# A Mamba-style scan block with attention and experts on one core: the exponent's "+ 1" on GpSimd, two matmul groups cut in thirds, two scan buffers exchanged and ten row loads issued earlier

## The reference

```python
x = x + L0(_gn(x), ...)            # group norm, then a 2-D selective scan
t = t + L1_attn(_ln_t(t), ...)     # linear attention (no softmax)
t = t + L1_ffn(_ln_t(t), ...)      # top-1 routing to 8 experts

# L0, B=4 images of 32x32 pixels, 384 channels, DI=192, N=16 states, K=4 directions
xz = x @ in_proj_w.T;  xh, z = split(xz)
xc = silu(depthwise_conv3x3(xh) + conv_b)
xs = stack(rows, columns, flipped rows, flipped columns)
dts, Bs, Cs = split(einsum(xs, x_proj_w))
dts = softplus(einsum(dts, dt_projs_w) + dt_projs_b)
h = h * exp(d_t * A) + (d_t * u_t) * B_t        # 1024 steps, for each of 16 states
y = sum_n h * C_t
...                                             # norm, gate by silu(z), out_proj
```

## Time and profile before

| what | value |
|---|---|
| median of 3 runs | 2448.16 us (2448.04 to 2449.8) |
| the profiled execution | 2452.28 us, its span 2450.4 us |
| busy: PE, DVE, ACT, POOL | 2047.7, 1642.5, 1139.7, 1283.9 us |
| mean granted clock of TensorE | 0.933 |
| first scan starts at | 306.38 us |

### The profile page before, as it was taken

One profiled execution on the slowest core, in us unless ns is written; L12 is line 12 of the kernel. 1 busy time (PEld: TensorE's weight loads), 2 busy tenths in 40 slices (PEclk: granted clock), 3 DMA queues, 4 the chain that ended last, 5 costly groups with the idle time before them and its releaser, 6 DMA issues.

```text
span 2450.4 us, 20397 instructions
## 1 busy us (share of the span) xinstructions
PE 2047.7 (84%) x5854; PEld 954.6 (39%) x5854; DVE 1642.5 (67%) x1531; ACT 1139.7 (47%) x1228; POOL 1283.9 (52%) x455
## 2 busy tenths in 40 slices
PE   7977478888888888888888888668999599999998
PEld 3432123333333333333333333225665255555554
DVE  5686899999999999999999999474455200000000
ACT  2675756666666666666666666121121111111111
POOL 0101089999999999999989999000133111111110
PEclk9987589999999999999999999788999799999999
DMA  5554533222432223322223220401122633322210
GB/s 202 183 191 126 201 99 81 60 60 60 104 89 60 60 60 102 90 61 60 60 77 94 68 69 17 194 26 39 52 78 99 246 115 116 113 107 101 99 61 6
DMA packets 78848, 231.96 MB, mean 95 GB/s; under 512 B 10783, under 2 KB 37009, under 8 KB 76880
## 3 DMA queue, kind: packets, MB, share of 16 engines
q1 hardware_dynamic: 72656, 214.39, 27.8%
q0 software_dynamic: 6144, 16.98, 1.9%
HBM read 169.24 MB, written 64.03 MB: 95 GB/s over the span
## 4 chain that ended last, share of the span: by engine, by line
PE 44%; DVE 31%; issue 15%; ACT 6%; DMA 1%; DVEq 1%; POOL 0%; SPq 0%; ACTq 0%; POOLq 0%
DVE arena L1469 16%; PE ps L1249 10%; PE ps L1261 10%; PE ps L1010 7%; DVE ps L1462 6%; ACT ps L725 3%; PE ps L999 3%; PE ps L1198 3%; PE ps L914 2%; DVE arena L1335 1%; PE ps L941 1%; PE ps L1149 1%; PE ps L1187 1%; PE ps L1127 1%; PE ps L1059 1%
## 5 line engine op out<-in xcount | busy, mean ns | idle before, releaser
L537 POOL TENSOR_TENSOR arena<-arena 128x2048 f32<-128x2048 f32 x192 | 869.1, 4527 | 85.7 <-DVE arena L1469 85.7
L1010 PE MATMUL ps<-arena 128*128 128x512 f32 x1536 | 763.7, 621 | 29.0 <-DVE arena L1439 25.6
L1469 DVE TENSOR_TENSOR_SCAN arena<-arena,ps 128x1024 f32<-128x1024 f32 x264 | 603.7, 2287 | 44.9 <-DVE ps L1462 23.3
L999 PE MATMUL ps<-arena 96*128 (+1 forms) x1296 | 358.9, 393 | 214.4 <-DVE arena L1469 193.1
L730 ACT ACTIVATE arena<-ps 128x1024 f32<-128x1024 f32 x384 | 391.3, 1019 | 307.8 <-PE ps L999 304.6
L1010 PEld LDWEIGHTS ps<-arena 128*128 128x128 f32 x1536 | 303.9, 199 | 297.3 <-issue 233.8
L520 POOL TENSOR_TENSOR arena<-arena 128x1024 f32<-128x1024 f32 x120 | 283.1, 2359 | 101.2 <-DMA arena<-b_rows 101.2
L999 PEld LDWEIGHTS ps<-arena 96*128 96x128 bf16 x1296 | 119.3, 100 | 545.4 <-DVE arena L1469 302.4
L1462 DVE TENSOR_TENSOR ps<-ps,arena 128x1024 f32<-128x1024 f32 x264 | 319.0, 1208 | 8.2 <-PE ps L999 5.2
L1761 DVE TENSOR_TENSOR arena<-ps,arena 128x384 f32<-128x384 f32 x32 | 17.9, 558 | 450.0 <-PE ps L1261 450.0
L725 ACT ACTIVATE arena<-arena 128x1024 f32<-128x1024 f32 x264 | 300.8, 1140 | 26.1 <-DVE arena L1469 22.4
(11 more groups left out here) (202 smaller groups left out, 1670.6 us busy)
## 6 DMA issues: line engine op xcount, KB each, us to landing
arena<-b_rows SPq DMA_DIRECT2D x240, 256.0 KB, 7.5
arena<-in_w SPq DMA_DIRECT2D x16, 2304.0 KB
delta<-arena SPq DMA_DIRECT2D x24, 512.0 KB, 2.9
delta_x<-arena SPq DMA_DIRECT2D x24, 512.0 KB, 3.7
arena<-delta SPq DMA_DIRECT2D x24, 512.0 KB, 3.6
arena<-delta_x SPq DMA_DIRECT2D x24, 512.0 KB, 4.6
arena<-in_xT SPq DMA_DIRECT2D x6, 1536.0 KB, 9.6
slot_in<-arena SPq DMA_DIRECT2D x8, 772.0 KB, 14.0
```

The costliest lines, as they stand in the source:

```text
L537: nc.gpsimd.tensor_tensor(hst[:, h:h + 2], hst[:, h:h + 2], c_sb[:, c:c + 2], ALU.mult).then_inc(p2_ok, 2)
L999: mm = pe.matmul(dst[:, h * 512:(h + 1) * 512], sel_lhs[0:BR, n], bc[0:BR, q % OJ // J, dr, m, h * 512:(h + 1) * 512], start=True, stop=True)
L1010: mm = pe.matmul(Y_PS[:, h * 512:(h + 1) * 512], ident, hst[:, u % HRING, h * 512:(h + 1) * 512], start=(u == 0), stop=(u == UN - 1))
L1469: nc.vector.tensor_tensor_scan(h, f, x, 0.0, ALU.mult, ALU.add).then_inc(sc_ok, 1)
```

## The change

1. `one_more` of every half moves to POOL, as a `tensor_scalar` from `u_mk` to `w_mk`. ACT loses twelve instructions and DVE twelve.
2. `in_proj` loops over the thirds outside and the halves inside, and with j = 0 waits for each third of the normalised image by itself. `x_proj(p, 0)` likewise waits for each of the three `conv_out` by itself.
3. ACT loads the table for sqrt ahead of its first wait for data.
4. `hst` and `c_sb` exchange places. DVE now waits for `bc_st` alone; ACT waits for `rows_st` before unit 0, and for the last delta stores (`dm_st`) before it copies C of unit 3.
5. SP issues the first five B rows, ten DMAs, after the stores of the last half but one of pair 1, ahead of the last half's two stores.

```diff
-        c_sb, hst = rs.take(RING, S), rs.take(HRING, S)
+        hst, c_sb = rs.take(HRING, S), rs.take(RING, S)
...
                     store_delta(p, i)
+                    if p == 1 and i == HALVES - 2:
+
+                        sp.wait_ge(z_st, 32 * NP)
+                        for u in POOL_UNITS[:XRING]:
+                            b_row(0, u)
...
-            sp.wait_ge(z_st, 32 * NP)
-            for k in range(2):
-                sp.wait_ge(bc_st[k], K * NP // 2 * PLACED)
-                sp.wait_ge(rows_st[k], K * NP // 2 * 16)
-            for i in range(MADE):
-                sp.wait_ge(dm_st[i], NP * HALVES // MADE * 32)
...
+            def one_more(p, i):
+                m = p * HALVES + i
+                pool.wait_ge(u_ok, m + 1)
+                if m >= 2:
+                    pool.wait_ge(pd_ok, m - 1)
+                nc.gpsimd.tensor_scalar(w_mk[p][:, m % 2], u_mk[:, m % MADE], 1.0, None, ALU.add).then_inc(w_ok, 1)
+
             for p in range(NP):
                 for j in range(J):
                     by_columns(p, j)
+                for s in range(HALVES):
+                    one_more(p, s)
...
+            nc.scalar.preload_act_table_set("sqrt_and_others")
             group_std(0)
...
-                        if s % 2 == 0:
-                            one_more(p, s)
...
+                    if first and u == 3:
+                        for i in range(MADE):
+                            act.wait_ge(dm_st[i], NP * HALVES // MADE * 32)
                     nc.scalar.activation(c_sb[:, u % RING], C_PS, ACT.Copy).then_inc(c_free, 1)
...
             act.wait_ge(z_st, 32 * NP)
-            act.wait_ge(pd_ok, NP * HALVES)
-            act.wait_ge(split_ok, 2 * K * NP)
+            for k in range(2):
+                act.wait_ge(rows_st[k], K * NP // 2 * 16)
...
-                if j == 0:
-                    pe.wait_ge(xn_ok, im + 1)
                 slot = slot_free("in", im, j)
-                for h in range(2):
-                    for t in range(CT):
+                for t in range(CT):
+                    if j == 0:
+                        pe.wait_ge(xn_ok, im * CT + (t + 1))
+                    for h in range(2):
...
-                for h in range(2):
-                    for j in range(J):
+                for j in range(J):
+                    if k == 0:
+                        pe.wait_ge(ev_free, p * FILLS + IN_P + (j + 1))
+                    for h in range(2):
...
-                if i % 2:
-                    dve.wait_ge(u_ok, m + 1)
-                    if m >= 2:
-                        dve.wait_ge(pd_ok, m - 1)
-                    chain.link(nc.vector.tensor_scalar(w, u, 1.0, None, ALU.add))
-                else:
-                    dve.wait_ge(w_ok, m // 2 + 1)
+                dve.wait_ge(w_ok, m + 1)
...
-            for i in range(MADE):
-                dve.wait_ge(dm_st[i], NP * HALVES // MADE * 32)
             for k in range(2):
                 dve.wait_ge(bc_st[k], K * NP // 2 * PLACED)
-                dve.wait_ge(rows_st[k], K * NP // 2 * 16)
```

More of the change, by code:

```diff
@@ L389, in load_delta, with b_row @@
                 sp.dma_start(dux[:, dr], du_dram[q * 2 + dr]).then_inc(du_ld[dr], 16)
+            def b_row(q, u):
+                dr, n = divmod(u, N)
+                x = q * len(POOL_UNITS) + pool_units(u)
+                if x >= XRING:
+                    old_q, old = divmod(x - XRING, len(POOL_UNITS))
+                    sp.wait_ge(sc_ok, old_q * UN + POOL_UNITS[old] + 3)
+                for im in range(2):
+                    sp.dma_start(xin[H2 * im:H2 * im + H2, x % XRING],
+                                 b_dram[q // J, dr, im * N + n].partition_broadcast(H2)).then_inc(b_ld[x % XRING], 16)
             for p in range(NP):
@@ L431, in _ @@
                     load_delta(half // 2, half % 2)
-                if U % UN in POOL_UNITS:
+                if U % UN in POOL_UNITS and U > POOL_UNITS[XRING - 1]:
                     b_row(U // UN, U % UN)
@@ L655, in exp_abs @@
                 nc.scalar.activation(u_mk[:, m % MADE], u_mk[:, m % MADE], ACT.Exp, scale=-1.0).then_inc(u_ok, 1)
-            def one_more(p, i):
-                m = p * HALVES + i
-                act.wait_ge(u_ok, m + 1)
-                if m >= 2:
-                    act.wait_ge(pd_ok, m - 1)
-                nc.scalar.activation(w_mk[p][:, m % 2], u_mk[:, m % MADE], ACT.Identity, bias=ones[:, 0:1]).then_inc(w_ok, 1)
             def log_w(p, i):
@@ L932, in x_proj @@
                 o, x = k % 2, p * K + k
-                if k == 0:
-                    pe.wait_ge(ev_free, p * FILLS + FILLS)
-                elif k == 1:
+                if k == 1:
                     pe.wait_ge(xT_ok, (p + 1) * J)
                 slot = slot_free("x", p, k)
-                for h in range(2):
-                    for j in range(J):
+                for j in range(J):
+                    if k == 0:
+                        pe.wait_ge(ev_free, p * FILLS + IN_P + (j + 1))
+                    for h in range(2):
                         mm = pe.matmul(slot[:, h * 512:(h + 1) * 512], xproj_w[:, k, j],
@@ L952, in delta_product @@
                 elif m == 1:
-                    pe.wait_ge(xn_ok, B)
+                    pe.wait_ge(xn_ok, B * CT)
                 for h in range(2):
@@ L1319, in normalise_x @@
                 for t in range(CT):
-                    ins = nc.vector.tensor_scalar(xt[:, r, t], xt[:, r, t], caff[:, im, t, 0:1], caff[:, im, t, 1:2], ALU.mult, ALU.add)
-                ins.then_inc(xn_ok, 1)
+                    nc.vector.tensor_scalar(xt[:, r, t], xt[:, r, t], caff[:, im, t, 0:1], caff[:, im, t, 1:2], ALU.mult, ALU.add).then_inc(xn_ok, 1)
             def taps(p, j):
```

1 line of the change is left out of this document (removed).

## The result

| | kernel before | changed kernel |
|---|---|---|
| median, 7 runs each | 2448.04 us (2447.06 to 2449.8) | 2458.26 us (2455.68 to 2461.25) |
| ratio | | 1.004, 95% interval 1.0028 to 1.0052 |
| profiled execution, span | 2452.28, 2450.4 us | 2458.26, 2456.5 us |

The changed kernel is slower by 10.2 us, 0.4%. The forecast was 2445.0 us, with a range up to 2457. Read against each other, the two profiles differ by 6.1 us only, because the profiled execution of before lies 4 us above its median.

The account below looks back on a forecast made before the run. DVE was taken to set the pace in both delta loops. Start -2.8, first x_proj of pair 1 -3.0, end -3.0, loops +4.4 and +1.2 make -3.2: 2448.2 - 3.2 = 2445.0 us, range 2437 to 2457.

Parts of the forecast that it names:

- T: Delta loops: time of POOL's new instruction for u + 1, taken as 1.2 us, half the two-input price of 2.36.
- its 15 steps: Delta loops: thirteen charges on DVE plus half 1 and half 0 of pair 1, each growing with T.
- I charge DVE T - 0.3: Delta loops: each POOL instruction falling into DVE's busy time lengthens DVE's work by T - 0.3 = 0.9 us.
- the third rival: Delta loops: charge on DVE not paid, as POOL gets its turn while DVE waits anyhow; 2434.4 us, chance 0.08.
- The start: Prologue, items 2 and 3: earlier table load -1.3 and in_proj by thirds -1.5, together -2.8 us.
- The first x_proj of pair 1: Item 2: two of three thirds run before the last conv_out; -3.7 us, less 0.7 for a cold clock, -3.0.
- The 0.7 us that I took off for a colder clock: Pair 1 after the first x_proj: next delta product in a cold stretch, second x_proj recovers only part; +0.7 us.
- The end: Last finish to fifth scan, items 4 and 5: fifth scan at 318.4 instead of 321.45, -3.0 us.
- Slow POOL: First rival, delta loops: T about 2.0, like POOL's copy, giving 2457 us; chance 0.28 for T above 1.4.
- The end that gives nothing: Fourth rival: row loads hold the last stores beyond 319.3 and ACT stalls DVE; 2448 us, chance 0.07.
- the fast POOL: Second rival, delta loops: POOL's instruction as fast as its memset, T = 0.9, giving 2440.8 us; chance 0.12.
- the charge that is not paid: The same as the third rival: POOL's instruction takes nothing from DVE in the delta loops; 2434.4 us, chance 0.08.

Follow-up runs that it names:

- POOL's prices alone: The kernel before plus twelve POOL instructions on spare columns at the start of POOL's program, each waited for; 2450.89 us in a single run.
- the run with two B rows ahead: The changed kernel with item 1 taken back and only two of the five B rows ahead of the last delta stores; 2440.48 us, 0.9963.

## Why the prediction was wrong

**What failed is the price of the new instruction.** The step is "From below: the memset ...; from above: TENSOR_TENSOR of the same shape, with two inputs, 2.36 us. I take half of the two-input price, T = 1.2 us". T is 2.77, above the bound that I called an upper one. It rested on the belief that one input cannot cost more than two; no row of the trace said so, and the row with POOL's prices alone says the contrary. The range's upper end, 2457, came from T = 2.0 and so was too low too. The 1.9 cycles an element that the Trainium skill gives (GPSIMD Engine Reference, section 7) make, as an estimate, 1.6 us, nearer than my value and still far below the 2.77 measured.

The price alone does not repair the forecast. The prediction's own sum, with its 15 steps, gives at T = 2.77 a time of 2445.0 + 15 x 1.57 = 2468.6 us, 10 us above the measured one: its rule for the charge would have missed on the other side.

**What stood in its place is a late w.** "I charge DVE T - 0.3" would be 2.5 us at the true T. Measured were 0.7 us for each charged operation, below the 0.9 that I used, but on 18 operations (16 du and 2 `split_lo`). Together they are 12.6 us, and the prediction's sum holds fourteen charges of 0.9, also 12.6 (it says thirteen elsewhere). The mean over the 96 operations of finish and lost part is 1.34 us, as forecast. This term came out right by luck: neither its rule nor its count holds.

What was wrong is "DVE sets the pace there". I added to DVE's work and let w come late only in half 1. With T = 2.77, w came late for 20 of 24 lost parts, 32.9 us in all; before, DVE had waited 14.2 us ahead of lost parts and 5.2 ahead of its own `one_more`. In part it was the chain of lost part, first finish operation, POOL, next lost part, which is then longer than DVE's work, and in part POOL's time behind ACT's exponent. The mechanism named against the third rival, that w must wait for `pd_ok` of half m-2, was right, but its consequence for the pace I did not work out. Where `pd_ok` comes last, POOL had to fit into the 2.5 us of DVE's last two operations, and this condition stood in no rival.

Shown: a reading instruction upon which nobody waits costs 6.0 us, the same with the wait 16.3, and the same waits with a link of 0.95 us that reads nothing leave no loss. A link of 2.34 us that holds DVE up for longer costs more, not less. How the 16.3 us divide between the price and the hold on DVE is not shown, as no run had the long link without the hold.

**By the terms.** The two loops, first lost part to last finish, took 84.8 and 84.9 us where 81.4 and 82.6 were forecast. Half 0 was put at zero and costs 1.7 us in each pair: from the first `split_rest` to the first lost part are 12.2 us in pair 0 and 8.3 in pair 1, before 10.5 and 6.6. So item 1 cost, in the traces, 6.4 and 8.5 us (10.2 against the usual loop) instead of 1.2 and 4.4. In the medians it is 16.3 alone and 18.4 to 19.5 on top of the others, against 5.6 forecast: 11 to 14 us, about the whole miss of 13.3.

**The start** was right: PE begins at 16.98 us instead of 19.42, -2.4 (1.3 + 1.5 = 2.8 forecast). That the loop of pair 0 is reached 3.55 us sooner is partly chance, as PE took 6.78 us for the twelve records instead of 7.82, and between 6.80 and 8.45 in the other profiles, old start or new, all at a granted clock of 1.00. The first `split_rest` came at 90.45 to 91.30 us with the old start and at 87.56 to 88.76 with the new one (without the run with POOL's prices, whose added instructions stand there): 2.7 us on average.

**The first x_proj of pair 1**: -3.7 came through. The 0.7 us that I took off for a colder clock are not seen between the two profiles: the stretch behind it, with the second x_proj, took 10.14 us before and 10.13 after. But over all the profiles they are there. The delta product behind the first x_proj, PE's line in the changed kernel and in the run with two B rows ahead:

```profile
215.53 1.98 PE L959 MATMUL ps<-arena 48*128 48x512 f32 x4 [1.56 <-ACT arena L641]
...
209.83 3.78 PE L959 MATMUL ps<-arena 48*128 48x512 f32 x4 [1.84 <-ACT arena L632]
```

The granted clock was 1.00 in the first and 0.50 in the second. The six profiles with the old x_proj all have 1.98 us here; of the eight with the new one four have 1.98 and four 3.78. The stretch was 8.57 to 10.14 us with the old x_proj, 9.9 on average, and 8.57 to 13.02 with the new one, 10.9 on average. The second x_proj within it took 5.42 us at a granted clock of 1.00 and 8.21 at a mean of 0.66. So the term of +0.7 us is supported, with a wide scatter, and its cause, less work of PE just before, stays argued.

**The end** gave -3.4 for -3.0, by the steps forecast: ACT's wait for the stores became the last one (6.12 us), and it goes when fewer rows stand ahead of them. Shifted by the later last finish (308.57 instead of 300.94), the forecast landing of 316.3 is 323.9, and ACT's copy started at 323.55. One part of the delay was not in the forecast: SP needs 6.4 us to issue ten row loads (306.54 to 312.95), so the last half's two stores are issued only at 312.99 and 313.62, 3 to 4 us after the last finish; how much of the wait is this and how much the queue was not separated.

In the medians items 2 and 3 are worth -7.1 (forecast -5.8), and items 4 and 5 -1.8 (forecast -3.0). That they make -9.3 together (forecast -8.8) is partly luck, as the two misses have opposite signs.

**The rivals.** "Slow POOL" was the nearest, with its sign turning at T = 1.4; it was given 0.28. The end that gives nothing, the fast POOL and the charge that is not paid have fallen.

## What to carry to other kernels

Price an instruction that the trace doesn't show by its own operation, not by the number of its inputs; where no row has it, the upper end is open, and the sign may hang on it. When a step goes to an engine that has nothing else to do, look first whether it stands in a loop of waits: add up the links from one use of its buffer to the next, and also the time from the step's input to its result, and compare them with the work of the engine that set the pace. An idle engine can cost twice, by its own slowness in the chain and by what its reads take from the neighbour, and the second is measured by an instruction beside, upon which nobody waits.

## What the runs showed of the hardware

- POOL, 128 partitions of fp32, alone: TENSOR_SCALAR (add of a constant) 2.77 us for 1024 columns and 1.49 for 512; TENSOR_TENSOR 1.26 for 512; COPY 0.61 for 512. From the other kernels, the shortest beside DVE: TENSOR_TENSOR 2.34 and memset 0.95 for 1024.
- In these runs, what POOL takes from a DVE operation of 1.22 us with two operands in SBUF does not follow the length of POOL's operation: 0.72 us beside the TENSOR_SCALAR of 2.77, 2.0 beside the TENSOR_TENSOR of 2.34, nothing beside the memset. The charge fell on 16 to 18 of the 24 du. POOL for its part is held up 0.96 us by the DVE operation that is running when it starts.
- SBUF — State Buffer of the Trainium skill (section SBUF: two separate sides) says that the one that comes second is blocked for the other's whole instruction, and that a write alone doesn't count. The memset agrees with it, and so does the TENSOR_TENSOR (in the period shown above it ran from 117.55 to 120.87 us, and DVE's du from 118.69 to 121.94, so that du ended 1.07 us after it, less than du needs alone); the TENSOR_SCALAR doesn't, with 0.72 of 2.77 us, and here the measurement decides.
